# Router logits as eight more columns of the attention output product, and 64-row products in place of padding

## The reference

```python
h = layernorm(x)                              # x after attention
router_logits = h @ gate_w.T                  # 8 experts
probs = softmax(router_logits)
topk_vals, topk_idx = top_k(probs, 2)
topk_vals = topk_vals / sum(topk_vals)
y_e = (silu(h @ w1[e].T) * (h @ w3[e].T)) @ w2[e].T    # w1, w3: 704x256, w2: 256x704
out = sum over the two experts of topk_val * y_e
```

## Time and profile before

| what | value |
|---|---|
| median of three runs | 559.87 us (554.78 to 560.05) |
| profiled execution, its own time | 557.6 us |
| its span in the profile | 555.8 us |
| PE busy | 510.9 us, 92% of the span |
| DVE, ACT, POOL busy | 64%, 50%, 32% |
| chain that ended last, share of PE | 77% |
| mean granted TensorE clock | 0.98 |

### The profile page before, as it was taken

How to read it: one execution, slowest core, us unless ns; L and a number is a source line. 1 busy time by engine, 2 the same in 40 slices (tenths; PEclk the granted TensorE clock), 3 DMA queues, 4 the chain that set the end, 5 groups by cost and what they waited for, 6 DMA issues and landing times.

```text
span 555.8 us, 9970 instructions
## 1 busy us (share of the span) xinstructions
PE 510.9 (92%) x3285; PEld 419.0 (75%) x3286; DVE 356.6 (64%) x871; ACT 278.4 (50%) x529; POOL 179.4 (32%) x236
## 2 busy tenths in 40 slices
PE   3998989989989998989999998798999999999994
PEld 1647877878968876767778886576888888888883
DVE  5875778557457336556668675456777777777761
ACT  1594544216123265556565563025666666666651
POOL 3016539971032032332223110310433333333332
PEclk9999999999999999899999999878999999999998
DMA  8999010000010069000000005851122222222111
GB/s 321 401 337 291 1 43 35 1 0 1 1 38 1 0 243 397 34 29 20 11 32 12 20 20 190 340 172 30 20 39 38 38 38 38 38 38 38 28 17 22
DMA packets 25813, 47.47 MB, mean 85 GB/s; under 512 B 2224, under 2 KB 21168, under 8 KB 25392
## 3 DMA queue, kind: packets, MB, share of 16 engines
q1 hardware_dynamic: 21408, 41.76, 21.2%
q0 software_dynamic: 4080, 5.15, 6.3%
q10 hardware_dynamic: 288, 0.08, 0.1%
HBM read 32.01 MB, written 14.98 MB: 85 GB/s over the span
## 4 chain that ended last, share of the span: by engine, by line
PE 77%; DVE 10%; ACT 5%; issue 5%; POOL 1%; DMA 1%; POOLq 0%; ACTq 0%; DVEq 0%
PE ps L1757 16%; PE ps L1777 11%; PE ps L1550 6%; PE ps L1648 5%; PE ps L1633 4%; PE ps L1448 4%; PE ps L1663 4%; PE ps L1606 4%; PE ps L1572 4%; PE ps L1765 3%; PE ps L1682 2%; PE ps L1610 2%; PE ps L1414 2%; PE ps L1532 1%; ACT work L777 1%
## 5 line engine op out<-in xcount | busy, mean ns | idle before, releaser
L1757 PE MATMUL ps<-split,xsT 128*128 128x512 f32 (+1 forms) x414 | 95.4, 384 | 1.1 <-DVE split L1355 1.0
L1757 PEld LDWEIGHTS ps<-split,xsT 128*128 128x128 f32 x414 | 75.8, 191 | 14.2 <-issue 1.2
L1355 DVE TENSOR_TENSOR split<-early,split 128x1408 fp32r<-128x1408 f32 x46 | 72.8, 1622 | 7.6 <-ACT split L843 7.2
L1777 PE MATMUL ps<-mid,work 128*128 x276 | 63.4, 379 | 0.8 <-ACT work L832 0.8
L843 ACT CAST split<-early 128x1408 fp32r x46 | 62.6, 1365 | 0.9 <-issue 0.9
L609 POOL TENSOR_TENSOR rstd<-mhalf 128x1 f32<-128x1 f32 x23 | 22.8, 993 | 120.4 <-ACT work L839 120.4
L1205 DVE TENSOR_REDUCE nmax<-ps 128x1 f32<-128x128 f32 (+7 forms) x64 | 45.4, 750 | 22.2 <-PE ps L1633 22.0
L1777 PEld LDWEIGHTS ps<-mid,work 128*128 128x128 f32 x276 | 52.0, 190 | 7.0 <-issue 1.0
L1337 DVE TENSOR_TENSOR work<-work,ps 128x704 f32<-128x704 f32 x23 | 20.4, 887 | 43.0 <-PE ps L1757 43.0
L828 ACT ACTIVATE work<-ps 128x704 f32<-128x704 f32 x22 | 16.7, 758 | 50.2 <-PE ps L1757 50.2
L777 ACT ACTIVATE work<-ps,nmax 128x128 f32<-128x128 f32 (+7 forms) x48 | 35.9, 750 | 2.9 <-DVE nmax L1205 2.9
(11 more groups left out here) (256 smaller groups left out, 1141.0 us busy)
## 6 DMA issues: line engine op xcount, KB each, us to landing
early<-m_w SPq DMA_DIRECT2D x16, 704.0 KB, 9.6
expert_in<-pad SPq DMA_DIRECT2D x8, 1040.0 KB, 12.4
mid<-m_w SPq DMA_DIRECT2D x8, 640.0 KB, 8.9
work<-expert_in SPq DMA_DIRECT2D x23, 130.0 KB, 2.9
early<-factors SPq DMA_DIRECT2D x1, 2048.0 KB, 11.6
early<-wq SPq DMA_DIRECT2D x1, 2048.0 KB, 16.3
mid<-f_w SPq DMA_DIRECT2D x1, 2048.0 KB, 20.6
rows<-x_in SPq DMA_DIRECT2D x4, 256.0 KB, 3.8
```

The costliest lines, as they stand in the source:

```text
L1355: V.tensor_tensor(lo, expert_w(e, w), hi.bitcast(F32), ALU.subtract).then_inc(s_wlo[w], 1)
L1757: last = mm(up_flat[:, c0:c1], xsT[px][b][:, k, :], split_w[pw][:, k, c0:c1], start=(k == 0 and px == pw), stop=(k == KD - 1 and px == 1))
L1777: last = mm(ps[:, 6, 0:D], eaT[:, b, c, :], we[:, c, :], start=(c == 0), stop=(c == IB - 1))
```

## The change

The gate is centred over the 256 features (its mean taken off), so that the layer norm's subtraction of the mean drops out of the logits. What is left is `x @ gate` times rstd, and x is the sum of x before attention and `z @ W_O`. So `W_O @ gate` is worked out once and stands as eight more columns beside W_O; `attention_out` gives the second part of the logits with the same four products, now 264 columns wide. The first part (`base_logit`) is worked out once from the normalised h of attention, which is there in feature-major form. All of this is put between the fills of the projections: `gate_sums` before fill 13, `wo_transposed` before fill 15, `gate_folded` before fill 19 on PE, `centre_gate` and `read_gate_fold` on DVE, two copies on ACT.

The choice is made on the logits before they are scaled (rstd is positive), right behind the variance. Only the difference of the two largest is scaled and goes to ACT for the exponential. `route_transposed`, `routed_feature_major`, `route_logits`, `route_max` and two steps of `route_choice` are gone; `route_counts` stands one step earlier. In the experts the sixth block has 64 rows and both memsets are gone.

```diff
-        wo_sb = view(work, 6144, QB, D)
+        wo_m = view(work, 6144, QB, D + E)
@@ GpSimd
-                if i == TT + 1:
-                    pool.wait_ge(s_pv, TT * HEADS // 2)
-                    nc.gpsimd.memset(mid[ILAST:P, :]..., 0.0).then_inc(s_w2pad, 1)
@@ ScalarE
+                if q == 17:
+                    act.wait_ge(s_woTp, 1)
+                    for k in range(KD):
+                        last = nc.scalar.copy(woT[:, k, :], ps[:, k, :])
+                    last.then_inc(s_woT, 1)
-                nc.scalar.copy(routed_T[:, i % 2], ps[:, 6 + i % 2, 0:D]).then_inc(s_rTc, 1)
-                nc.scalar.activation(prob_e[:, i, :], ps[:, 6 + i % 2, D:D + E], ACT.Exp, ...)
+                nc.scalar.activation(prob_e[:, i, 0:TOP], prob_e[:, i, 0:TOP], ACT.Exp).then_inc(s_lexp, 1)
@@ VectorE, order in the attention loop
-                if rel == 0 and i >= 2:
-                    route_normalise(i - 2)
-                if rel == 1 and i >= 2:
-                    route_choice(i - 2)
                 if rel == 3 and 1 <= i <= TT:
                     add_attention(i - 1)
                     route_variance(i - 1)
+                    route_choice(i - 1)
                 if rel == 0 and i >= 2:
-                    route_max(i - 2)
+                    route_normalise(i - 2)
+                    route_difference(i - 2)
+                    route_slots(i - 2)
                 if rel == 1 and i >= 2:
-                    route_tail(i - 2)
-                    route_slots(i - 2)
+                    route_weights(i - 2)
@@ TensorE
+            def gate_sums():
+                for k in range(KD):
+                    last = mm(ps[:, 0, 0:E], ones, gate_sb[:, k, :], start=(k == 0), stop=(k == KD - 1))
+            def wo_transposed():
+                for k in range(KD):
+                    for c in range(QB):
+                        last = nc.tensor.transpose(ps[:, k, c * P:(c + 1) * P], wo_m[:, c, k * P:(k + 1) * P], ident)
+            def gate_folded():
+                for c in range(QB):
+                    for k in range(KD):
+                        mm(ps[:, 0, c * E:(c + 1) * E], woT[:, k, c * P:(c + 1) * P], gate_sb[:, k, :], ...)
+                for t in range(TT):
+                    at = (QB + t) * E
+                    for part, (pw, ph) in enumerate(W_PARTS):
+                        for k in range(KD):
+                            last = mm(ps[:, 0, at:at + E], hT_split[ph][:, k, t * P:(t + 1) * P], gate_r[:, pw, k, :], ...)
-                    last = mm(ps[:, 6 + i % 2, 0:D], zT[:, c, :], wo_sb[:, c, :], ...)
+                    last = mm(ps[:, 6 + i % 2, 0:D + E], zT[:, c, :], wo_m[:, c, :], ...)
@@ TensorE, expert_aT
-                    last = nc.tensor.transpose(ps[:, 4 + c // 4, (c % 4) * P:(c % 4 + 1) * P],
-                                               ea[:, b, c * P:(c + 1) * P], ident)
+                    w = P if c < IB - 1 else ILAST
+                    last = nc.tensor.transpose(ps[0:w, 4 + c // 4, (c % 4) * P:(c % 4 + 1) * P],
+                                               ea[:, b, c * P:c * P + w], ident)
@@ TensorE, expert_down
-                    last = mm(ps[:, 6, 0:D], eaT[:, b, c, :], we[:, c, :], start=(c == 0), stop=(c == IB - 1))
+                    w = P if c < IB - 1 else ILAST
+                    last = mm(ps[:, 6, 0:D], eaT[0:w, b, c, :], we[0:w, c, :], start=(c == 0), stop=(c == IB - 1))
```

More of the change, by code:

```diff
@@ L215, in build @@
         w_first, w_second = bias_sb[:, 0:24], bias_sb[:, 24:48]
+        base_logit = view(bias_sb, 0, TT, E)
+        spread = rs_t[:, 0:TT]
         dest_now = slot_i_t[:, 0:2]
@@ L278, in build @@
         s_zT, s_ao, s_x3 = sem("zT"), sem("attn_out"), sem("x3")
-        s_rT, s_rTc, s_lg, s_lmax, s_lexp, s_chosen, s_cnt = (sem(n) for n in (
-            "routed_transposed", "routed_T", "logits", "logit_max", "logit_exp", "chosen", "counts"))
+        s_ldiff, s_lexp, s_chosen, s_cnt = (sem(n) for n in (
+            "logit_difference", "logit_exp", "chosen", "counts"))
+        s_gsum, s_gc, s_woTp, s_woT, s_fold, s_folded = (sem(n) for n in (
+            "gate_summed", "gate_centred", "wo_transposed", "wo_T", "gate_folded", "gate_fold_read"))
         s_slots, s_scat, s_table, s_dest = sem("slots"), sem("scattered"), sem("tile_table"), sem("destinations")
@@ L823, in _ @@
                     attend(2 * m + 1)
+                if rel == 0 and i >= 2:
+                    logits_exp(i - 2)
             def expert_silu(i):
@@ L1681, in attention_out @@
                 for c in range(QB):
-                    last = mm(ps[:, 6 + i % 2, 0:D], zT[:, c, :], wo_sb[:, c, :], start=(c == 0), stop=(c == QB - 1))
+                    last = mm(ps[:, 6 + i % 2, 0:D + E], zT[:, c, :], wo_m[:, c, :], start=(c == 0),
+                              stop=(c == QB - 1))
                 last.then_inc(s_ao, 1)
-            pe.wait_ge(s_wo, 16)
-            def route_transposed(i):
-                if i == TT - 1:
-                    keep_busy(16, 0)
-                pe.wait_ge(s_hh, TT * PH_MOE + i + 1)
-                for k in range(KD):
-                    last = nc.tensor.transpose(ps[:, 6 + i % 2, k * P:(k + 1) * P], hh[:, i, k * P:(k + 1) * P], ident)
-                last.then_inc(s_rT, 1)
-            def route_logits(i):
-                pe.wait_ge(s_rTc, i + 1)
-                for k in range(KD):
-                    last = mm(ps[:, 6 + i % 2, D:D + E], routed_T[:, i % 2, k * P:(k + 1) * P], gate_sb[:, k, :],
-                              start=(k == 0), stop=(k == KD - 1))
-                last.then_inc(s_lg, 1)
             def route_counts(i):
                 if i == TT - 1:
-                    keep_busy(14, 0)
+                    keep_busy(20, 0)
                 pe.wait_ge(s_chosen, i + 1)
@@ L1732, in _ @@
                     attended(m - 2)
-                if rel == 0 and i >= 2:
-                    route_logits(i - 2)
                 if WIDE // 2 <= m < STEPS:
```

104 lines of the change are left out of this document (61 added, 43 removed).

## The result

The changed kernel is **slower**: 571.29 us median (four runs, 568.84 to 574.06), against 557.61 (554.78 to 560.05) for the kernel before beside it, a ratio of 1.0238 with a 95% interval of 1.0195 to 1.0282. That it is slower is clear; whether by more or less than 2% is not. The forecast was 568.7 in 558 to 577. The profiled execution took 571.78, its span is 569.9, 14.2 longer than before.

What follows compares the result with a forecast made beforehand. PE's list was taken as the bound, without gaps in most stretches, with the end of attention also bound by the load queue. Terms 7.9 - 6.5 - 3.2 + 12.9 = +11.1 on 557.6 gave 568.7 us, range 558 to 577.

Steps and rivals of the forecast that it cites:

- Projections, +7.9: Projections: the fold's 68 narrow products (7.0) and eight transposes (0.87) add 7.9 us, uncovered; bounds 3.5 and 11.
- the third rival: Projections: the clock falls in the fold's narrow products, price 1.7 to 3.4 us, total 571 to 572; chance 0.12.
- Attention loop, -6.5: Six routings inside the attention loop: transposes, `route_logits` and PE's waits go, saving 6.5 us; bounds 3.7 and 8.5.
- End of attention, -3.2: End of attention and start of experts: last store of x releases ACT, PE gets weights 3.2 us earlier; bounds 0, -6.
- Slot stores long done: End of attention: sign that the slot stores finish well before the last store of x lets ACT's casts go.
- `keep_busy` inside: End of attention: shortened `keep_busy` lists lie inside the time already counted and give nothing more.
- Experts, +12.9: Experts: 64-row product (0.31) and 64-column transpose (0.25) change format, 0.56 us a tile, 23 times: 12.9; bounds 0 and 15.4.
- The column format: Experts: the transpose with 64 output rows costs 0.25 us a tile for going into and out of its format.
- The sum: Whole kernel: 7.9 - 6.5 - 3.2 + 12.9 = +11.1 us, giving 568.7 us, 2.0% more.

Runs made afterwards that it cites:

- the last version: Changed kernel with full sixth block, fold in six parts, loads reordered, 40 `keep_busy` products ahead, third slot load before w2, later w2 wait: 551.51 us, ratio 0.9876.

## Why the prediction was right, and where it was not

**Projections, +7.9: the passes right, the clock missed.** The price of a narrow pass held: 0.106 against 0.103. Without the clock the fold cost 8.3, and 8.6 in parts (49.2 less 40.6). The 8.3 is 54.7 less 40.6, less 5.1 (the 10.2 us at 0.50, from 201.1 to 211.4, did the work of 5.1), less 0.7 for a spell of half clock (some us at 0.50, at places that differ between executions) at the first fills, which the execution with the store moved did not have (54.1). The 5.1 is the step that failed: the third rival, given 0.12 and a price of 1.7 to 3.4, came true. "PE never stands still there" was the reason against it, and it did not count: PE was busy for 11.60 of 11.60 us up to 199.1, and the clock fell at 201.1. The clock fell in each of the three traces that have the fold in one piece (after, the full sixth block, the store moved) and in none of the five with it in parts. The prediction stopped this rival at the end of the fold, while the fills behind it, until 211.4, ran at half clock too. The measured 14.1 lies above the term's upper bound of 11.

**Attention loop, -6.5: right.** Measured -6.2. The waits for the choice (1.6) and the normalised row (0.5) are gone. Some 0.9 of it belongs to a spell of half clock that the trace before had at 222.8; against the kernel with the 64-row product alone, whose attention had none, it is -5.3. That lies in the bounds of 3.7 to 8.5.

**End of attention, -3.2: right in size and bound.** Measured -3.8. The last store of x let ACT go, as the prediction said; the chain of the run with the full sixth block shows it with 14.5 us. "Slot stores long done" was wrong: their rows were held up by the same full DMA engines (each took 5.7 us or more to land), with their load issued 1.6 us ahead of ACT's release. Nor was `keep_busy` inside: with the store out of the way it is what ends last. Both lie close behind the bound, so moving the store alone gave 2.8.

**Experts, +12.9: half of it right.** The 64-row product cost 0.34 a tile for 0.31 in the prediction (2.88 for 2.58 and 0.28 for 0.22, by the starts to the nanosecond 0.344), 7.9 over 23 tiles; the run that has it alone gave 6.4 by medians and 8.5 by the ratio (by its interval 5.0 to 12.0), the run that takes it out, transposes included, 8.9 and 7.5. The column format, 0.25 a tile and 5.8 us, did not come. It was read from `attended`, where the narrow instructions are products. The two runs with one product more show 0.23 and 0.32 for a lone product of that format, so the price was right and was put on an operation that does not pay it. Why a transpose does not is open. The stretch shows 5.8 in place of 7.9 mostly since the trace before had a spell of half clock at its second tile, worth 1.7; the 0.4 that are left are open.

The Trainium skill, "TensorEngine Tiling (Array Packing)", Key Properties, says that a change of the tiling mode drains the engine. The trace agrees for 64-row and 64-column products, at 0.34 and 0.23 to 0.32 us for the way in and out, and differs for the 64-column transpose, which cost nothing in 23 tiles; there the measurement decides. By "TensorE: Matmul & The Clock Gate", Why this matters for your kernels, a single product of K=32 takes as long as one of K=128, and by that the term would be 0. The runs show 0.34 a tile. By the starts it stands in four places: 0.09 ahead of the first 64-row pass, 0.10 between its two passes, 0.09 behind the second, and 0.06 behind the first transpose.

**The sum** was right partly by luck: 5.8 too much for the transposes stood against 5.1 too little for the clock. The remaining +4.3 ahead of the first fill is no effect of the change; two of the spells of half clock, at 44 and 126, worth 1.7 each, account for most of it. The run with the store moved and the last version had none there, and their first fill came at 158.3 and 157.9. Such spells are also why one kernel's runs spread over 5 us: beside these experiments the kernel before took 554.1 to 556.0 in the executions with a mean clock of 0.989 or more and 557.5 to 562.2 in those with 0.981 or less.

Not tried: taking ACT's wait for the last store of x away. Its reason is not the additions to the same rows in memory, as the description of the kernel has it: POOL, which issues them, has a wait of its own. The place into which ACT rounds the first weights is shared with the last tile of x, from which the store reads.

## What to carry to other kernels

In a list of TensorE without gaps, cutting a full product down to 64 rows to save padding costs time: it streams as many columns, and going into the format and out of it cost 0.34 us each time, 0.23 to 0.32 for a product cut to 64 output rows. A transpose cut to 64 output rows cost nothing and gained nothing. Narrow products should be handed out between wide ones rather than stand in a row: the same 64 passes cost 5 us more in one piece. And when work before a transfer-bound joint becomes shorter, read the order of the queue again. Here the loads needed last stood ahead of the rows needed first, the store moved alone uncovered the next bound after 2.8 us, the 40 products moved alone only shifted the wait, and with all of it in place the kernel took 551.5 us against 559.1 for the kernel before.

## What was unexpected of the hardware

- The granted clock fell to 0.50 with PE busy without a break, 3.7 us after the first narrow product of the fold (197.42 to 201.13), and stayed there for 10.2 us, 3.9 of them under products of 512 columns.
- A lone transpose with 64 output rows between full ones costs nothing (period 7.27 with it and without), a product of the same format 0.32 in two passes and 0.23 in one.
- Over 354 to 376 us the DMA share was 1.02 at 401 GB/s, and a store of 128 rows of 256 numbers issued behind the loads landed after 14.9 us; in the kernel before the like store took 10.6.
